# Mixture-of-experts tail of a decoder layer: second layer with its weights stationary, the next rows turned ahead

## The reference, cut to what matters

```python
capacity = int(0.5 * 3200 / 8)                   # 200 slots for each expert
probs = softmax(x @ w_switch + b_switch); pmax = probs.max(-1); routes = probs.argmax(-1)
pos = rank of the token among those of its expert; keep = pos < capacity
slot = where(keep, routes * capacity + pos, E * capacity)
buf_e = zeros.at[slot].set(x).reshape(E, capacity, 256)
h = relu(einsum('ecd,edh->ech', buf_e, w1) + b1)     # 200 x 256 by 256 x 1024
y = einsum('ech,ehd->ecd', h, w2) + b2               # 200 x 1024 by 1024 x 256
out = where(keep, y[slot], x) * (pmax / pmax)
x = layernorm(x + out)
```

## Time and profile before

| | us |
|---|---|
| median of three runs | 1565.06 |
| the three runs | 1562.82, 1565.06, 1567.44 |
| the profiled execution | 1558.71 |
| its span | 1556.9 |
| mean granted clock of TensorE in it | 0.896 of full speed |

### The profile page before, as it was taken

One profiled execution on the slowest core, in us unless ns is written; L12 is line 12 of the kernel. 1 busy time (PEld: TensorE's weight loads), 2 busy tenths in 40 slices (PEclk: granted clock), 3 DMA queues, 4 the chain that ended last, 5 costly groups with the idle time before them and its releaser, 6 DMA issues.

```text
span 1556.9 us, 33968 instructions
## 1 busy us (share of the span) xinstructions
PE 1203.6 (77%) x11098; PEld 873.9 (56%) x11098; DVE 831.7 (53%) x2482; ACT 669.1 (43%) x1611; POOL 335.0 (22%) x485
## 2 busy tenths in 40 slices
PE   3577877877888888888878888888878887775886
PEld 2354555555555555555555656565555555554774
DVE  4235555555655565555556555555555555543432
ACT  0124544445545444444445544444455454532110
POOL 2111221222222222222222222222222222210111
PEclk8668999999999999999999999999999999876998
DMA  4233333333333333333333333333333333206542
GB/s 157 47 80 83 83 73 86 86 75 84 81 71 78 75 83 76 84 84 84 84 84 84 80 73 82 72 84 84 78 77 81 71 78 74 66 18 214 194 148 72
DMA packets 187012, 134.99 MB, mean 87 GB/s; under 512 B 95798, under 2 KB 182762, under 8 KB 186734
## 3 DMA queue, kind: packets, MB, share of 16 engines
q1 hardware_dynamic: 181778, 127.50, 33.5%
q0 software_dynamic: 3200, 6.61, 1.4%
q10 hardware_dynamic: 1984, 0.23, 0.1%
HBM read 91.06 MB, written 43.00 MB: 86 GB/s over the span
## 4 chain that ended last, share of the span: by engine, by line
PE 38%; DMA 28%; SPq 9%; issue 9%; DVE 7%; POOL 4%; ACT 4%; DVEq 0%; POOLq 0%; ACTq 0%
DMA query_halves<-Qhl 8%; DMA self_stack<-self_halves 8%; DMA self_halves<-QKhl 6%; DMA Qst<-query_halves 5%; PE MI L1006 4%; POOL QKhl L701 4%; PE MI L809 4%; SPq L574 4%; PE MX L1123 4%; PE MI L810 3%; PE MX L837 3%; PE ST L993 3%; SPq L590 3%; PE MX L843 2%; PE ST L870 2%
## 5 line engine op out<-in xcount | busy, mean ns | idle before, releaser
L1427 DVE TENSOR_REDUCE negmax_x<-MX 100x1 bf16<-100x361 f32 x512 | 260.0, 532 | 123.8 <-PE MX L975 119.1
L1192 ACT ACTIVATE wide<-ST 128x800 f32<-128x800 f32 (+1 forms) x256 | 171.0, 669 | 222.7 <-PE ST L993 221.9
L975 PE MATMUL MX<-stacked,Qst 96*128 96x361 f16 x512 | 152.1, 327 | 40.3 <-DMA Qst<-query_halves 29.9
L707 POOL TENSOR_TENSOR Qhl<-Qx,Qhl 128x400 f16<-128x400 f32 x32 | 30.2, 944 | 695.0 <-ACT Qhl L1264 695.0
L837 PE MATMUL MX<-mask_q,identb 100*128 100x400 bf16 (+1 forms) x128 | 57.1, 547 | 93.8 <-DMA self_stack<-self_halves 92.4
L993 PE MATMUL ST<-Qst,stacked 112*128 112x200 f16 x768 | 124.5, 278 | 0.3 <-ACT wide L1192 0.3
L975 PEld LDWEIGHTS MX<-stacked,Qst 96*128 96x128 f16 x512 | 50.7, 102 | 101.8 <-issue 54.7
L701 POOL TENSOR_TENSOR QKhl<-QK,QKhl 128x900 f16<-128x900 f32 x32 | 60.5, 1891 | 204.9 <-ACT QKhl L1199 204.9
L1154 ACT ACTIVATE early<-MI,bkC 128x361 f32<-128x361 f32 x64 | 36.0, 562 | 148.8 <-PE MI L810 145.5
L993 PEld LDWEIGHTS ST<-Qst,stacked 112*128 112x128 f16 x768 | 72.5, 109 | 41.2 <-issue 26.2
L1398 DVE TENSOR_SCALAR QK<-MI,small,parity_s 128x100 f32<-128x100 f32 x128 | 42.6, 374 | 76.9 <-PE MI L810 72.9
(11 more groups left out here) (259 smaller groups left out, 2918.4 us busy)
## 6 DMA issues: line engine op xcount, KB each, us to landing
stacked<-key_halves SPq DMA_DIRECT2D x96, 180.5 KB, 4.1
self_halves<-QKhl SPq DMA_DIRECT2D x32, 450.0 KB, 2.9
cT<-in_cT SPq DMA_DIRECT2D x32, 361.0 KB, 4.0
key_halves<-Khl SPq DMA_DIRECT2D x32, 361.0 KB, 2.7
self_stack<-self_halves SPq DMA_DIRECT2D x64, 150.0 KB, 3.9
Qst<-query_halves SPq DMA_DIRECT2D x96, 100.0 KB, 2.6
early<-in_w SPq DMA_DIRECT2D x8, 1024.0 KB
self_stack<-self_halves SPq DMA_DIRECT2D x32, 225.0 KB, 3.8
```

The costliest lines, as they stand in the source:

```text
L975: pe.matmul(MX[:, n % 2, 0:M], Qst[p][0:96, n * S:n * S + 128], Kst[p][0:96, n // 2 * M:(n // 2 + 1) * M], start=True, stop=True).then_inc ...
L1192: act.activation(cross_part(Px, u), ST[0:n, first:first + 2, 0:width], ACT.Exp).then_inc(st_exp, 1)
L1427: dve.tensor_reduce(negmax_x[:, n:n + 1], MX[0:S, n % 2, 0:M], X, ALU.max, negate=True).then_inc(max_read, 1)
```

## The change

1. Layer 2 exchanges its operands: a 128x128 block of W2 is stationary and the 200 slots of `hT` stream, so the result comes out turned, as two halves of 128 channels by 200 slots.
2. VectorE copies that result to the new tile `yT`, in one copy of 128x400. TensorE turns it back with four transposes into the PSUM bank `MI[1]` (`turned_back`), in the next expert, between steps q = 1 and q = 2 of its layer 1. What VectorE did behind layer 2 (bias, residual, norm) is now `rows_done`: for expert e it stands in the list of expert e+1, behind the relu of q = 3. The relus, and the four small operations on `e_top`, stay where they were; the two token conversions move into `rows_done`.
3. The rows of expert e+1 are turned in expert e, between its layers 1 and 2 (`rows_turned`), and ScalarE copies them out there (`rows_out`); `XeT` has two buffers. On ScalarE the rstd of expert e-1 comes behind that copy.
4. SyncE issues for each expert now: W1 (behind layer 1 of expert e-2), b1 (behind its relus), W2 (behind its layer 2), then the rows (behind `e_sum` of e-2, as before), then b2 (behind `y_ok` of e-2), which has a semaphore of its own.
5. The loops on TensorE and ScalarE lose their last round, experts 6 and 7 are written out, and behind expert 7 stand `turned_back` and `rows_done` once more.

```diff
@@ -363,7 +363,8 @@
         b1 = [sb(f"b1{p}", [128, 8]) for p in range(2)]
         b2 = [sb(f"b2{p}", [S, D]) for p in range(2)]
         Xe = [part(wide, 2000 + 2 * WIDE * p, [S, 2, WIDE]) for p in range(2)]
-        XeT = part(wide, 1600, [128, 2, CAP])
+        XeT = [part(wide, 1600, [128, 2, CAP]), part(cT[0].rearrange("p k m -> p (k m)"), 0, [128, 2, CAP])]
+        yT = part(cT[1].rearrange("p k m -> p (k m)"), 0, [128, 2, CAP])
         hT = part(wide, 0, [128, 8, CAP])
         Y = [part(wide, 3040 + 512 * p, [S, 2, D]) for p in range(2)]
         e_top = sb("e_top", [S, 2])
@@ -452,6 +453,7 @@
         t_pos = sem("t_pos")
         scattered = sem("scattered")
         w_in = [sem(f"w_in{p}") for p in range(2)]
+        b_in = [sem(f"b_in{p}") for p in range(2)]
         xe_in = [sem(f"xe_in{p}") for p in range(2)]
         xe_mm = sem("xe_mm")
         xe_ok = sem("xe_ok")
@@ -459,6 +461,8 @@
         h_act = sem("h_act")
         h_dve = sem("h_dve")
         y_mm = sem("y_mm")
+        yt_ok = sem("yt_ok")
+        y_tr = sem("y_tr")
         y_ok = sem("y_ok")
         y_out = sem("y_out")
         e_slot = sem("e_slot")
@@ -617,14 +621,24 @@
 
             def load_weights(e):
                 p, n = e.parity, e.index()
-
-                after = held(sp, e.done(per=2, back=2))
+                hidden, summed = held(sp, e.done(per=4, back=2)), held(sp, e.done(per=2, back=2))
                 sp.wait_ge(started, 1)
-                sp.wait_ge(y_ok, after)
+                sp.wait_ge(h_mm, hidden)
                 sp.dma_start(W1[p][:], io["w1"][bass.ds(n, 1)].rearrange("a (k p) f -> p (a k) f", p=128)).then_inc(w_in[p], 16)
+                sp.wait_ge(started, 1)
+                sp.wait_ge(h_act, summed)
+                sp.wait_ge(h_dve, summed)
+                sp.dma_start(b1[p][:], io["b1"][bass.ds(n, 1)].rearrange("a p f -> p (a f)")).then_inc(w_in[p], 16)
+                sp.wait_ge(started, 1)
+                sp.wait_ge(y_mm, summed)
                 sp.dma_start(W2[p][:], io["w2"][bass.ds(n, 1)].rearrange("a (k p) f -> p (a k) f", p=128)).then_inc(w_in[p], 16)
-                sp.dma_start(b1[p][:], io["b1"][bass.ds(n, 1)].rearrange("a p f -> p (a f)")).then_inc(w_in[p], 16)
-                sp.dma_start(b2[p][:], io["b2"][bass.ds(n, 1)].rearrange("a f -> (a f)").partition_broadcast(S)).then_inc(w_in[p], 16)
+
+            def load_bias(e):
+                p, n = e.parity, e.index()
+                added = held(sp, e.done(per=2, back=2))
+                sp.wait_ge(started, 1)
+                sp.wait_ge(y_ok, added)
+                sp.dma_start(b2[p][:], io["b2"][bass.ds(n, 1)].rearrange("a f -> (a f)").partition_broadcast(S)).then_inc(b_in[p], 16)
 
             def load_rows(e):
                 p, n = e.parity, e.index()
@@ -641,14 +655,17 @@
             sp.wait_ge(scattered, 16 * B)
             load_rows(Seq(0))
             load_rows(Seq(1))
+            load_bias(Seq(0))
+            load_bias(Seq(1))
             for n in range(0, B, 8):
                 sp.wait_ge(d_dve, n // 8 + 1)
                 sp.wait_ge(d_act, n // 8 + 1)
                 sp.dma_start(io["out"][n * S:(n + 8) * S, :].rearrange("(n p) d -> p n d", p=S), x2_all[:, n:n + 8]).then_inc(d_out, 16)
             with sp.Fori(0, (E - 2) // 2) as j:
                 for n in (2, 3):
+                    load_weights(Seq(n, j))
                     load_rows(Seq(n, j))
-                    load_weights(Seq(n, j))
+                    load_bias(Seq(n, j))
 
             sp.wait_ge(d_out, 16 * (B // 8))
             sp.wait_ge(y_out, 32 * E)
@@ -1097,7 +1114,7 @@
             iterations(pe, body)
 
 
-            def expert(e):
+            def rows_turned(e):
                 p = e.parity
                 pe.wait_ge(xe_in[p], e.pairs(16))
                 pe.wait_ge(xe_ok, e.done(back=1))
@@ -1106,28 +1123,47 @@
                         mm = pe.transpose(MI[0][:, k * CAP + s * S:k * CAP + (s + 1) * S], Xe[p][:, s, k * 128:(k + 1) * 128],
                                           ident[0:S, 0:S])
                 mm.then_inc(xe_mm, 1)
+
+            def turned_back(e):
+                pe.wait_ge(yt_ok, e.done())
+                pe.wait_ge(y_ok, e.done(per=2, back=1))
+                for s in range(2):
+                    for t in range(2):
+                        mm = pe.transpose(MI[1][0:S, s * D + t * 128:s * D + (t + 1) * 128], yT[:, t, s * S:(s + 1) * S], ident[:])
+                mm.then_inc(y_tr, 1)
+
+            def expert(e, first=False, last=False):
+                p = e.parity
                 pe.wait_ge(xe_ok, e.done())
-                pe.wait_ge(w_in[p], e.pairs(64))
+                pe.wait_ge(w_in[p], e.pairs(48))
                 for q in range(4):
 
                     pe.wait_ge(h_act if q % 2 == 0 else h_dve, e.done(per=2, k=q // 2 + 1, back=1))
                     for m in (2 * q, 2 * q + 1):
                         mm = two(ST[:, q, m % 2 * CAP:(m % 2 + 1) * CAP], lambda k: W1[p][:, k, m * 128:(m + 1) * 128],
-                                 lambda k: XeT[:, k])
+                                 lambda k: XeT[p][:, k])
                     mm.then_inc(h_mm, 1)
+                    if q == 1 and not first:
+                        turned_back(Seq(e.n - 1, e.j))
+                if not last:
+                    rows_turned(Seq(e.n + 1, e.j))
                 pe.wait_ge(h_act, e.done(per=2))
                 pe.wait_ge(h_dve, e.done(per=2))
-                pe.wait_ge(y_ok, e.done(per=2, back=1))
-                for s in range(2):
+                pe.wait_ge(yt_ok, e.done(back=1))
+                for t in range(2):
                     for m in range(8):
-                        mm = pe.matmul(MX[0:S, s, 0:D], hT[:, m, s * S:(s + 1) * S], W2[p][:, m], start=(m == 0), stop=(m == 7))
+                        mm = pe.matmul(MX[:, t, 0:CAP], W2[p][:, m, t * 128:(t + 1) * 128], hT[:, m], start=(m == 0), stop=(m == 7))
                     mm.then_inc(y_mm, 1)
 
-            expert(Seq(0))
+            rows_turned(Seq(0))
+            expert(Seq(0), first=True)
             expert(Seq(1))
-            with pe.Fori(0, (E - 2) // 2) as j:
+            with pe.Fori(0, (E - 4) // 2) as j:
                 expert(Seq(2, j))
                 expert(Seq(3, j))
+            expert(Seq(E - 2))
+            expert(Seq(E - 1), last=True)
+            turned_back(Seq(E - 1))
 
 
         @block.scalar
@@ -1328,13 +1364,13 @@
                 act.wait_ge(e_rs, e.done(per=2, k=1))
                 act.activation(rs3[:], ln3[:], ACT.Exp, scale=-0.5).then_inc(e_rs, 1)
 
-            def expert(e, first=False):
+            def rows_out(e):
+                act.wait_ge(xe_mm, e.done())
+                act.wait_ge(h_mm, e.done(per=4, back=2))
+                act.activation(XeT[e.parity], MI[0][:, 0:2 * CAP].rearrange("p (k c) -> p k c", k=2), ACT.Copy).then_inc(xe_ok, 1)
+
+            def expert(e, first=False, last=False):
                 p = e.parity
-                act.wait_ge(xe_mm, e.done())
-                act.wait_ge(h_mm, e.done(per=4, back=1))
-                act.activation(XeT[:], MI[0][:, 0:2 * CAP].rearrange("p (k c) -> p k c", k=2), ACT.Copy).then_inc(xe_ok, 1)
-                if not first:
-                    rstd_rows(Seq(e.n - 1, e.j))
                 for q in (0, 2):
                     act.wait_ge(h_mm, e.done(per=4, k=q + 1))
                     if q == 0:
@@ -1342,12 +1378,19 @@
                     for m in (2 * q, 2 * q + 1):
                         ins = act.activation(hT[:, m], ST[:, q, m % 2 * CAP:(m % 2 + 1) * CAP], ACT.Relu, bias=b1[p][:, m:m + 1])
                     ins.then_inc(h_act, 1)
-
+                if not last:
+                    rows_out(Seq(e.n + 1, e.j))
+                if not first:
+                    rstd_rows(Seq(e.n - 1, e.j))
+
+            rows_out(Seq(0))
             expert(Seq(0), first=True)
             expert(Seq(1))
-            with act.Fori(0, (E - 2) // 2) as j:
+            with act.Fori(0, (E - 4) // 2) as j:
                 expert(Seq(2, j))
                 expert(Seq(3, j))
+            expert(Seq(E - 2))
+            expert(Seq(E - 1), last=True)
             rstd_rows(Seq(E - 1))
 
 
@@ -1632,29 +1675,15 @@
                     ins.then_inc(d_dve, 1)
 
 
-            def expert(e):
+            def rows_done(e):
                 p = e.parity
-                dve.wait_ge(xe_in[p], e.pairs(16))
+                dve.wait_ge(y_tr, e.done())
+                dve.wait_ge(b_in[p], e.pairs(16))
                 dve.wait_ge(y_out, e.done(per=32, back=2))
-                dve.tensor_scalar(e_top[:], Xe[p][:, :, D], 1.0, None, ALU.max).then_inc(e_slot, 1)
                 for s in range(2):
                     dve.tensor_scalar(token[p][s][:], Xe[p][:, s, D + 1:WIDE], NOWHERE, None, ALU.add)
-                dve.wait_ge(e_slot, e.done(per=4, k=1))
-                dve.reciprocal(e_max[:], e_top[:]).then_inc(e_slot, 1)
```

(40 more changed lines are left out.)

## The result

The changed kernel takes 1596.52 us in the median (1590.6 to 1602.26, four runs), against 1563.94 for the kernel before in the same comparison: the ratio is 1.0217, 95% interval 1.0184 to 1.0249. It is slower, clear of noise; whether by more than 2% the interval leaves open. The median lies 0.5 us from the time forecast.

The account below looks back on a forecast made before the run. TensorE's own order was taken to bound the expert block. The terms -19.7 - 1.5 + 3.5 + 35.8 + 11.9 + 1.7 = +31.7 on 1565.06 gave 1596.8, written as 1596 us; range 1581 to 1607.

Parts of the forecast that it names:

- A: Layer 2 with 200 streaming columns: layer 2 to next layer 1 falls, -19.7 us over seven; last layer 2 shorter, -1.5.
- B: Four transposes turning layer 2's result back inside layer 1 of experts 1 to 7: 0.5 us each time, +3.5 us.
- C: Before layer 2 of experts 1 to 6, TensorE waits for the late load of the next rows: +35.8 us.
- D: TensorE's clock drops in each of six waits for rows, slowing the work behind: 1.98 us each, +11.9 us.
- E: Tail behind the last layer 2: PSUM copy, four transposes, tokens, additions and hand-overs take 2.03 us, +1.7 us.
- F: ScalarE's rstd order, b2's own semaphore, written-out rounds and SyncE's new load order: no cost.
- Rival 1: TensorE still waits for the rows but its clock holds or returns at once: +19.8, 1585 us; chance 0.10.
- Rival 2: The rows are there when TensorE asks before layer 2, no wait: -16.0, 1549 us; chance 0.03.
- Rival 3: The rows' load stands behind 1 MB of weights in SyncE's queue: +17, 1613 us; chance 0.08.

Follow-up runs that it names:

- third buffer: The changed kernel with a third buffer for the rows, asked for a whole expert before TensorE turns them, expert loops written out: 1547.81 us, ratio 0.9918.
- earlier sum: The changed kernel with VectorE's tokens, b2 and residual of the expert before moved between its relus of q = 1 and q = 3: 1566.09 us.
- filled wait: The changed kernel with 28 unneeded matmuls of 128x112 added in front of each of TensorE's six waits for the rows: 1582.35 us.
- weights by layer alone: The kernel before with only the new order of the loads (W1, b1, W2, then rows, then b2): 1563.22 us, ratio 1.0002.
- written-out kernel: The changed kernel with its expert loops written out on SyncE, TensorE and VectorE, and nothing else: 1589.34 us, ratio 1.0156.
- fastest version: The third buffer kernel, with TensorE waiting for the relu of q = 3 only before layer 2's seventh matmul: 1541.80 us, ratio 0.9860.

## Why the prediction was right

All six terms can be read from the block of the profile after, and they add up to its 31.6 us. "From runs" says what else bears the term out. The mechanism came as forecast. That the median came within 0.5 us is luck in part: the forecast time stood on 1565.06 us for the kernel before, its own comparison has 1563.94, and the four executions of the changed kernel spread over 12 us.

| step | forecast | measured | how |
|---|---|---|---|
| A layer 2 to next layer 1, seven times | -19.7 | -19.3 | 5.49 us warm (1445.06 to 1450.55) against 8.24 |
| A last layer 2 | -1.5 | -1.5 | 5.65 against 7.12 |
| B turned back, seven times | +3.5 | +2.4 | layer 1 takes 6.01 against 5.67 |
| C wait for the rows, six times | +35.8 | +33.0 | gap 6.40 in the mean against 0.90; from runs: gone with the third buffer, 17 us shorter with the earlier sum |
| D the clock behind it, six times | +11.9 | +15.0 | layer 2 to layer 1 7.98 in the mean against 5.49; from runs: 15.2 (filled wait) |
| E tail | +1.7 | +2.0 | 15.0 from the end of the last layer 2 to the end of the span, 13.0 before |
| F loads in a new order | 0 | 0 | weights by layer alone, block +0.1 |

A, B and the whole wait chain of C stand as the steps put them: the load is issued 2.61 us behind layer 1's end (1456.56 to 1459.17; 2.59 to 2.61 in all six) where 2.77 was worked out. Rival 1 (the clock holds) fell with the 7.97 to 8.31 us of each layer 2 behind a wait. Rival 2 (the rows are there in time) was argued away beforehand from VectorE's part of that chain, and the six waits bear that out. Rival 3 (the load stands behind weights) fell too: the six loads took 2.8 to 3.2 us to their reader.

Two sizes were off, and they cancel. The load was taken from the earlier trace rows with 3.39 us from issue to reader; measured the same way the six have 3.08 in the mean (2.84 to 3.23), which is 1.9 of the 2.8 us that C came out lower. VectorE's part, 2.60 for 2.77, is another 1.0, and the transposes gave 0.1 back. The prediction's estimate of 2.55 us with the fixed cost of the Trainium skill (DMA: Bandwidth & Descriptors, Anatomy of one DMA) lies below all six; that section fits DMAs issued on the GpSimd path, and this load is SyncE's. The clock's price was taken from the cold layer 1 of the earlier trace rows, 1.98 us; measured 2.49 each. That layer starts 2.2 us behind the transposes that had already put TensorE to work (1422.30 to 1424.54), while here layer 2 follows its transposes within 0.72 us, so more of it ran at 1.2 GHz. The clock came back 5.5 to 6.2 us behind the restart, as the 6.0 us of the earlier trace rows had it, which I had kept for the upper end. B was less than I took: 0.34 us for four transposes between matmuls, where the row of four by themselves had 0.51, which counts the overlap with the next matmul. E's size was right and its path only in part: VectorE's last scaling starts 1.8 us later behind the last layer 2 than before (4.57 for 2.79), as forecast, but GpSimd is then still busy with expert 6's rows, and the chain that ended last goes over the four scatters of experts 6 and 7. That is the other 0.2 us.

Where the expected gain went can now be said in numbers. Both ideas of the change are good: together, without the wait, they are worth 16.6 us (third buffer), turning ahead alone 9.7, the exchange with its turning back alone 6.4. The place of the sum turned the -16.6 into +31.6: by the changed kernel's own trace 33.0 us of TensorE waiting and 15.0 of TensorE slow afterwards.

## What to carry to other kernels

When an epilogue is put off into the next iteration, look at everything that it releases, not only at what it needs: a buffer that it frees is refilled that much later. If the reader of that buffer is moved earlier in the same edit, the two moves add up against each other, and one more buffer (or the reader behind the work that covered it) settles it. A wait of some 6 us on TensorE must be priced with the slower clock behind it, here nearly half as much again. And where a run fills a wait with work, read from its trace whether the work or the wait ended last.

## What the runs showed of the hardware

- The granted clock fell in all six idle stretches of 5.4 to 5.8 us of the changed kernel and was down when the transposes started; it came back 5.5 to 6.2 us behind the restart and cost 2.49 us each. In the written-out kernel it fell in all six stretches of 5.2 to 5.6 us too, but layer 2 took anything from 6.69 to 8.35 us behind them, 1.0 to 2.7 more than the 5.65 with the clock up: the price of one wait is not a constant.
- With gaps of 2.9 to 3.7 us (the earlier sum) the clock was still up at the end of every gap and fell early in every other layer 2 behind them; the price was 1.68 us. Work that nobody needs, in the gap, keeps it up and gave back 15.2 us over six waits.
- Four float32 transposes between two matmul groups add 0.34 us inside layer 1 and 0.35 between the layers of the fastest version. Where TensorE waits for the relu anyway they are free: the gap is 0.90 us with them (third buffer, expert 0) and without (expert 7).
- The time to the first layer 1, in code that is all but the same, differs by up to 12 us between the profiled executions of the ten kernels, while the block of the kernel before and of the one with the loads in a new order agree within 0.1 us (132.4 and 132.5).
- With `rows_done` of experts 6 and 7 close together the end is bound by GpSimd: the four scatters of these two experts follow each other at 3.6 to 3.7 us (1584.19, 1587.83, 1591.56, 1595.15 in the changed kernel), each behind the landing of the one before. From the end of the last layer 2 to the end of the span it takes 15.0 us in the changed kernel, 15.9 in the fastest version and 13.0 before.
